# x as two float16 pieces turned by DMA, projections as three float16 products, mask turned by DMA, q read by ScalarE

## The reference

```python
xn = layernorm(x)
q = (xn @ Wq.T + bq) * 0.25; k, v = split(xn @ Wkv.T + bkv)        # 16 wide each
q = q.reshape(16, 16 * 512, 16)                                     # a plain reshape
attn = softmax(q @ k.T) @ v;  out = heads_back(attn) @ Wo.T + bo
gates = one_hot_of_the_best(xn @ w_gate)                            # 6 experts, top 1
tokens = A @ B                                                      # (6, 100, 256)
p = softmax((xn @ tokens.T) / 16)
delta = ((p @ (tokens @ wt.T + wt_b)) + xn) @ wd.T + wd_b, times scale
ffn = xn + log(sum_e exp(delta_e) * gates_e)
result = x + out + ffn
```

## Time and profile before

| | |
|---|---|
| median of 3 runs | 976.48 us (974.66 to 976.85) |
| span of the profiled execution | 972.5 us; no other time of it is given, and the median lies 4.0 us above the span |
| TensorE busy | 907.7 us (93%) |
| VectorE busy | 808.2 us (83%) |
| ScalarE busy | 682.1 us (70%) |
| GpSimd busy | 459.1 us (47%) |
| chain that ended last | TensorE 75%, VectorE 6%, DMA 6%, ScalarE 6%, GpSimd 3% |
| DMA | 76.07 MB, 78 GB/s on average |

### The profile page before, as it was taken

The page is one execution under the profiler, slowest core; times in us unless marked ns, Lnnn a source line. Parts: engine busy times, 40 slices in busy tenths (PEclk is TensorE's granted clock), DMA queues, the critical chain, the costliest instruction groups (busy, mean ns, idle before and its releaser), DMA issues.

```text
span 972.5 us, 17720 instructions
## 1 busy us (share of the span) xinstructions
PE 907.7 (93%) x5868; PEld 354.1 (36%) x5868; DVE 808.2 (83%) x1556; ACT 682.1 (70%) x1380; POOL 459.1 (47%) x567
## 2 busy tenths in 40 slices
PE   4889999999999999999999999999999999998976
PEld 3433333333434333343334333333333334332323
DVE  5688978889898888989888898989889898888814
ACT  1217777877777777777777777777777777777791
POOL 3654545554554555455444655444465544524200
PEclk9779999999999999999999999999999999999998
DMA  4230232422324242422423242242423223241120
GB/s 118 70 59 31 76 67 71 91 87 81 91 72 100 63 98 79 95 76 83 88 84 79 89 91 69 91 82 93 88 71 91 81 76 84 71 90 46 58 66 33
DMA packets 86192, 76.07 MB, mean 78 GB/s; under 512 B 18263, under 2 KB 70232, under 8 KB 86104
## 3 DMA queue, kind: packets, MB, share of 16 engines
q1 hardware_dynamic: 86104, 74.94, 29.9%
HBM read 39.28 MB, written 33.54 MB: 75 GB/s over the span
## 4 chain that ended last, share of the span: by engine, by line
PE 75%; DVE 6%; DMA 6%; ACT 6%; POOL 3%; issue 2%; SPq 2%; POOLq 0%; DVEq 0%
PE pO L349 22%; PE pA L331 14%; PE pB L336 8%; PE pA L470 6%; PE pA L412 6%; PE pA L488 5%; DVE M L750 3%; DMA o_parts<-OTr 3%; ACT P L597 3%; PE pA L472 3%; PE pA L402 3%; PE pB L392 2%; SPq L937 2%; PE pA L443 2%; DMA Rb<-l_parts 2%
## 5 line engine op out<-in xcount | busy, mean ns | idle before, releaser
L750 DVE TENSOR_REDUCE M<-pA 128x1 f32<-128x512 f32 x1024 | 652.4, 680 | 82.7 <-PE pA L331 80.9
L597 ACT ACTIVATE P<-pB 128x512 f32<-128x512 f32 x1002 | 553.5, 599 | 147.6 <-PE pB L336 143.1
L331 PE MATMUL pA<-K,Q 48*128 48x512 f16 x1024 | 316.8, 387 | 19.9 <-DVE M L750 10.3
L336 PE MATMUL pB<-Q,K 50*128 50x512 f16 x1002 | 307.3, 383 | 0.3 <-ACT P L597 0.3
L349 PE MATMUL pO<-P,VK 128*32 128x512 f32 x2048 | 272.8, 605 | 11.1 <-ACT P L597 7.9
L331 PEld LDWEIGHTS pA<-K,Q 48*128 48x128 f16 x1024 | 64.0, 94 | 323.2 <-DVE M L750 243.8
L887 POOL TENSOR_TENSOR On<-Op,Rb 128x512 f32<-128x512 f32 x31 | 39.9, 1288 | 146.9 <-DMA Rb<-l_parts 104.7
L873 POOL TENSOR_SCALAR Cz<-Cx 128x512 f32<-128x512 f32 x32 | 62.0, 1936 | 50.4 <-ACT Cx L579 50.4
L349 PEld LDWEIGHTS pO<-P,VK 128*32 128x32 f32 x2048 | 40.4, 108 | 108.3 <-issue 82.2
L412 PE MATMUL pA<-xT,wq 128*128 128x256 f32 x256 | 74.1, 416 | 1.3 <-ACT xT L541 0.7
L488 PE MATMUL pA<-wo,On 128*128 128x256 f32 x248 | 69.9, 407 | 4.3 <-DVE RL L763 2.5
(11 more groups left out here) (130 smaller groups left out, 865.7 us busy)
## 6 DMA issues: line engine op xcount, KB each, us to landing
o_parts<-OTr SPq DMA_DIRECT2D x62, 256.0 KB, 2.3
Q<-q_pieces SPq DMA_DIRECT2D x90, 128.0 KB, 4.1
X<-in_x SPq DMA_DIRECT2D x16, 512.0 KB, 3.9
q_pieces<-Qp SPq DMA_DIRECT2D x32, 256.0 KB, 2.1
out<-OUT SPq DMA_DIRECT2D x32, 256.0 KB, 3.1
Op<-o_parts SPq DMA_DIRECT2D x31, 256.0 KB
Rb<-l_parts SPq DMA_DIRECT2D x31, 256.0 KB
K<-KS SPq DMA_DIRECT2D x96, 16.0 KB, 1.8
```

The lines of the kernel that those rows point to most:

```text
L331: e.matmul(bank1("ab", t)[:, :], Q16[r:r + 48, b % 2, h, 128 * s:128 * s + 128], K16[r:r + 48, b % 3, :], start=True, stop=True).then_inc( ...
L336: e.matmul(bankB(t)[:, :], K16[r:r + 50, b % 3, 128 * i:128 * i + 128], Q16[r:r + 50, b % 2, :, 32 * hh:32 * hh + 32], start=True, stop=Tr ...
L597: e.activation(P[:, u % PR, :], bankB(u + LB)[:, :], ACT.Exp, scale=alpha).then_inc(S("e"))
L750: e.tensor_reduce(M[:, t // 32 % 2, t % 2, t % 32 // 2:t % 32 // 2 + 1], bank1("ab", t)[:, :], AX, ALU.max, negate=True).then_inc(S("mx"))
```

## The change

Each batch's normalised x is written by GpSimd times 1024 as a high and a low float16 piece (XP); SP issues one transposing DMA per batch that turns both pieces into xT (two for batch 0). The weights are scaled and split into two float16 pieces once (`scl`, `scd`). Every projection from x is three float16 products (high-high, high-low, low-high), over 512 columns at once for uk and q. The factors are taken out again where the results are read. The mask is turned by a DMA (`mkd`) instead of by TensorE and ScalarE. ScalarE reads q. The residual is worked out from x, not from XN. Slots are moved.

```diff
+PIECES = ((0, 0), (0, 1), (1, 0))
+    "root": -91.4, "refine": -90.2, "norm": -87.2, "pieces": -84.2, "xtd": -74.2,
+    "residual": 2.3, "q0": -57, "qe0": -55.4, "qs0": -53.8, "qw0": -50.2, "uk": -53, "uke": -51.4, "ks": -50.2,
+    "kd": -46.2, "vg": -49, "vge": -48.3, "q1": -45, "qe1": -43.4, "qs1": -42.2, "qw1": -38.2,
+    "vt": -41.1, "vte": -40.4, "gate": -38.8, "mask": -36.6, "mkd": -34.2,
-    "d0": -1, "dexp0": -0.4, "d1": 7, "dexp1": 7.6, "guard0": 8.8, "dlog0": 13.2, "radd0": 14.8,
+    "d0": -1, "dexp0": -0.4, "d1": 23, "dexp1": 23.6, "guard0": 24.8, "dlog0": 29.2, "radd0": 30.8,
-    "o0": 131, "fo0": 131.6, "o1": 163, "fo1": 163.6, "st0": 165.2, "o2": 179, "fo2": 179.6, "o3": 183,
+    "o0": 131, "fo0": 131.6, "o1": 155, "fo1": 155.6, "st0": 157.2, "o2": 163, "fo2": 163.6, "o3": 183,
...
+                        w.wait_ge(S(f"xt_{b % 2}"), turned(b))
+                        for k, (wp, xp) in enumerate(PIECES):
+                            for c in range(2):
+                                mm = e.matmul(bank1(f"q{g}", b)[:, :], wqP[:, wp, c, 128 * g:128 * g + 128],
+                                              xT[:, b % 2, :, xp, c, :], start=(k == 0 and c == 0), stop=(k == 2 and c == 1))
...
-                        for c in range(2):
-                            e.matmul(dst, xT[:, b % 2, c, 128 * t:128 * t + 128], wc[:, c, 0:C],
-                                     start=(c == 0), stop=False)
+                        for k, (wp, xp) in enumerate(PIECES):
+                            for c in range(2):
+                                e.matmul(dst, xT[:, b % 2, t, xp, c, :], wcP[:, wp, c, 0:C],
+                                         start=(k == 0 and c == 0), stop=False)
...
+                        e.activation(qf[:, g, :], bank1(f"q{g}", b)[:, :], ACT.Identity, scale=scl[:, 5:6],
+                                     bias=bq_s[:, g:g + 1]).then_inc(S(f"qe{g}"))
...
+                if (b := due("pieces", n)):
+                    w.wait_ge(S("xn"), 4 * b + 4)
+                    w.wait_ge(S(f"xt_{(b - 1) % 2}"), turned(b - 1))
+                    e.tensor_copy(XP[:, :, 0, :], XN[:, :, :]).then_inc(S("xh"))
+                    w.wait_ge(S("xh"), b)
+                    e.tensor_tensor(XP[:, :, 1, :], XN[:, :, :], XP[:, :, 0, :], ALU.subtract).then_inc(S("xl"))
...
+                if (b := due("xtd", n)) is not None:
+                    w.wait_ge(S("d"), 4 * (b - 1))
+                    if b:
+                        w.wait_ge(S("xl"), b)
+                    for i0, i1 in ((0, 2), (2, 4)) if b == 0 else ((0, 4),):
+                        if b == 0:
+                            w.wait_ge(S("xl0"), i1 // 2)
+                        e.dma_start_transpose(xT[:, b % 2, i0:i1].rearrange("p i k c t -> p (i k c) t"),
+                                              XP[:, i0:i1].rearrange("p i k n -> p (i k n)")).then_inc(S(f"xt_{b % 2}"), 16)
+
+                if (b := due("mkd", n)) is not None:
+                    w.wait_ge(S("mk"), b + 1)
+                    w.wait_ge(S("mk1"), 1)
+                    w.wait_ge(S("mm"), b)
+                    w.wait_ge(S("utm"), b)
+                    e.dma_start_transpose(mkT[:, :].rearrange("p (i t) -> p i t", t=128),
+                                          mk[:, :, :].rearrange("p i n -> p (i n)")).then_inc(S("mkd"), 16)
```

More of the change, by code:

```diff
@@ L73 @@
 PARTH = {"lr": 66.2, "or": 66.3, "rec": 68.8, "lw": 69.4, "rb": 72.2, "on": 78.3}
[L75 to L78, removed]
+PE_NAMES = ("ab", "pv", "rg", "bs", "bw0", "bw1", "w2", "uk", "q0", "q1", "vg", "vt", "s", "p", "a", "d0", "d1",
+            "d2", "d3", "mt", "o0", "o1", "o2", "o3", "sl0", "sl1", "oa0", "oa1", "oa2", "oa3", "ob0", "ob1", "ob2", "ob3")
+ACT_NAMES = ("root", "alpha", "bwe0", "bwe1", "w2e", "pieces", "qe0", "qe1", "vge", "vte", "sexp", "pte", "dexp0",
              "dexp1", "dexp2", "dexp3", "dlog0", "dlog1", "mte", "ex", "ot")
-DVE_NAMES = ("rng", "two", "scl", "stats0", "stats1", "stats2", "stats3", "aggr", "refine", "uke0",
-             "uke1", "qe00", "qe01", "qe10", "qe11", "gate", "smax", "ssum", "mm", "mx", "rec", "fo0", "fo1", "fo2",
+DVE_NAMES = ("rng", "two", "scl", "scd", "stats0", "stats1", "stats2", "stats3", "aggr", "refine", "pieces", "uke",
+             "gate", "smax", "ssum", "mm", "mx", "rec", "fo0", "fo1", "fo2",
              "fo3", "nl00", "nl01", "nl02", "nl03", "nl10", "nl11", "nl12", "nl13")
-POOL_NAMES = ("var", "refine", "norm", "residual", "ks", "qs0", "qs1", "mask", "utm", "snorm", "guard0", "guard1", "radd0",
+POOL_NAMES = ("var", "refine", "norm", "pieces", "w2s", "residual", "ks", "qs0", "qs1", "mask", "utm", "snorm", "guard0", "guard1", "radd0",
               "radd1", "ms", "on")
-SP_NAMES = ("load", "kd", "qw0", "qw1", "qread", "md", "ow", "lr", "or", "lw", "rb", "st0", "st1")
+SP_NAMES = ("load", "xtd", "mkd", "kd", "qw0", "qw1", "qread", "md", "ow", "lr", "or", "lw", "rb", "st0", "st1")
 def slots():
@@ L362, in _ @@
                     w.wait_ge(*before1("bs", 0))
-                    w.wait_ge(S("ones"), 5)
+                    w.wait_ge(S("ones"), 4)
                     w.wait_ge(S("two"), 1)
-                    e.matmul(bank1("bs", 0)[:, 0:3], one[:, :], fac[:, 0:3], start=True, stop=True).then_inc(S("bs"))
+                    e.matmul(bank1("bs", 0)[:, 0:7], one[:, :], fac[:, 0:7], start=True, stop=True).then_inc(S("bs"))
                 for h in range(2):
@@ new lines, in _ @@
+                for g in range(2):
+                    if (b := due(f"q{g}", n)) is not None:
+                        w.wait_ge(*before1(f"q{g}", b))
+                        w.wait_ge(S(f"xt_{b % 2}"), turned(b))
+                        w.wait_ge(S("wqp"), 2)
+                        for k, (wp, xp) in enumerate(PIECES):
+                            for c in range(2):
+                                mm = e.matmul(bank1(f"q{g}", b)[:, :], wqP[:, wp, c, 128 * g:128 * g + 128],
+                                              xT[:, b % 2, :, xp, c, :], start=(k == 0 and c == 0), stop=(k == 2 and c == 1))
@@ L417, in _ @@
                     w.wait_ge(*before2("vg", b))
-                    w.wait_ge(S("xte"), 2 * b + 2)
-                    for c in range(2):
-                        for i in range(4):
-                            mm = e.matmul(bank2("vg", b)[32 * i:32 * i + 32, 0:128], wc[:, c, V0:V0 + 32],
-                                          xT[:, b % 2, c, 128 * i:128 * i + 128], start=(c == 0), stop=(c == 1))
+                    w.wait_ge(S(f"xt_{b % 2}"), turned(b))
+                    w.wait_ge(S("wcp"), 2)
+                    for k, (wp, xp) in enumerate(PIECES):
+                        for c in range(2):
+                            for i in range(4):
+                                mm = e.matmul(bank2("vg", b)[32 * i:32 * i + 32, 0:128], wcP[:, wp, c, V0:V0 + 32],
+                                              xT[:, b % 2, i, xp, c, :], start=(k == 0 and c == 0), stop=(k == 2 and c == 1))
                     mm.then_inc(S("vg"))
@@ L428, in _ @@
                     e.transpose(bank2("vt", b)[:, 0:128], VGs[:, :], idf[:, :]).then_inc(S("vt"))
-                if (b := due("mk", n)) is not None:
-                    w.wait_ge(*before2("mk", b))
-                    w.wait_ge(S("mk"), b + 1)
-                    o = bank2("mk", b)[:, :].bitcast(BF16)
-                    for i in range(4):
-                        mm = e.transpose(o[0:ER, 128 * i:128 * i + 128], mk[:, i, :], idb[:, :])
-                    mm.then_inc(S("mkt"))
                 if (b := due("s", n)) is not None:
@@ L547, in _ @@
                     e.activation(VGs[:, :], bank2("vg", b)[:, 0:128], ACT.Identity,
-                                 bias=vgb[:, 0:1]).then_inc(S("vge"))
+                                 scale=scl[:, 4:5], bias=vgb[:, 0:1]).then_inc(S("vge"))
                 if (b := due("vte", n)) is not None:
@@ L556, in _ @@
                     e.copy(G[:, :, :], o[:, :, D:D + NE]).then_inc(S("gt"))
-                if (b := due("mke", n)) is not None:
-                    w.wait_ge(S("mkt"), b + 1)
-                    w.wait_ge(S("mm"), b)
-                    w.wait_ge(S("utm"), b)
-                    e.copy(mkT[0:ER, :], bank2("mk", b)[0:ER, :].bitcast(BF16)[:, 0:T]).then_inc(S("mke"))
                 if (b := due("sexp", n)) is not None:
```

243 lines of the change are left out of this document (137 added, 106 removed), and 7 rows, old and new, of tables (FIRST, SLOT).

## The result

The changed kernel takes 1034.57 us (median; 1032.56 to 1039.72), the kernel before on the same chip 975.57: a ratio of 1.0617, interval 1.0578 to 1.0655. The forecast was 943 us. Its span is 1030.8 us.

A forecast was written before the change was run, and what follows sets the result against it. TensorE's order of work was taken to bound a batch, VectorE about 5 us behind. Per batch -4.2 + 0.6 + 0.5 = -3.1; span 972.5 + 13 (start) - 46.5 = 939, with 4.0 more 943 us; range 918 to 984.

The forecast's parts named there:

- the turned DMAs: SP's queue: x's turn lands in 5 us, hidden under 13; Rb queued behind it is charged 0.5 us a batch.
- TensorE, -4.2 us a batch: TensorE's products: turns of x and mask go, q, uk and delta get cheaper in f16; -4.2 us a batch, to 50.7.
- rival 3: TensorE: f16 products don't stream at one column a cycle (weight loads); 4.1 us a batch at the end, about 972; chance 0.07.
- VectorE, 47.0: VectorE per batch: four q reads go, two uk reads become one at 0.689; busy time falls from 49.2 to 47.0 us.
- Rival 2: VectorE becomes the bound, 47.0 against TensorE's 50.7; 2 us a batch instead of 0.6, 963 us; chance 0.16.
- The 0.6 us for its order: Allowance per batch for places where VectorE runs behind TensorE, such as slots 12 to 15 and 56 to 59.
- ScalarE at most 0.78 for q's read: ScalarE: each of two q reads of 512 columns takes 0.78 us at most; net -0.2 a batch, counted as nothing.
- GpSimd, hidden: GpSimd between normalisation and En: +4.2 us a batch, pieces 0.611 and 1.155 per half; 1.6 us cover left, nothing charged.
- The turned x in 5 us: x's transposing DMA, 512 KB a batch, lands in 5 us, near the 3.9 of the plain load of equal size.
- Rival 1: Turned x late, or holding up what queues behind it, at q or output projection; about 1045 at 20 us; chance 0.19.
- Start, first pair near 44, batch 1's q near 54: Start: batch 0's q at about 25 us, first pair about 44, batch 1's q near 54; charged +13 us (8 to 20).
- Period 52.9: Time of one batch in the long middle, forecast 52.9 us after 55.99; wrong if above 54.

The follow-up runs named there:

- e14: Changed kernel with one unused tile of 416 bytes a partition ahead of xT, so Q16 begins at 70656, a multiple of 512: 985.4 us (1.0123).
- e13: e4 with one unused tile of 416 bytes a partition ahead of xT, so Q16 begins at 70656, a multiple of 512: 966.68 us (0.9924).
- e3: Changed kernel with batch 0's read of q put behind the turning of batch 0's mask on SP's queue: 1026.16 us (1.0533).
- e1: Changed kernel with kd, the six DMAs that place k, moved back to slot 23.8, behind the read of the softmax sums: 1018.35 us (1.0447).
- e4: Changed kernel with both moves, e1's of kd and e3's of batch 0's read of q: 1012.59 us (1.04).
- e9: Kernel before with one unused tile of 32 bytes a partition ahead of xT, so Q16 begins at 70176: 994.57 us (1.0228).
- e16: Kernel before with Q16 alone 32 bytes further (70176), every other tile at its place modulo 512: 997.37 us (1.0247).
- e5: e4 with the transposing DMAs of x and mask replaced by plain DMAs between the same tiles, nothing turned: 1008.96 us (1.0342).
- e18: e13 with the reciprocal and its result's write two slots later, and x's transposing DMA behind Rb: 985.63 us (1.0093).

## Why the prediction was wrong

The account of the 59 us, by the runs: the place of the tiles 49 (changed kernel against e14; Q16's, as argued above), the two slots on SP's queue 19 (e14 against e13: the first mask 8 by e3, so kd about 11 by difference; e1's 16 with e3's 8 make 24, e4 gives 22, so they overlap a little), and -7 to -9 for all the rest of the change (e13 against the kernel before in the same runs and in the first), against the -33 forecast.

- **What the prediction left out, and what decided:** it has no term for where the tiles lie. In its part on what bounds the kernel and in its turned DMAs, q's reads and o_parts stay as they were. They became 1.1 us slower, o_parts behind them 1.0 to 1.7 in the rows above, and its landing decides when VectorE may go on with the row maxima. In the kernel before Rc idled there too, 0.65 to 2.3 us, but TensorE waited for maxima at L331 for 3.4 us only between 160 and 880; the same misplacement made that 15.4 (e9) and cost 20 to 22 us (e9, e16). In the changed kernel the wait went from 31.4 (e14) to 52.5, and the mean clock from 1.00 to 0.96, where e9 still has 0.99. That these two, more of each wait and the half clock behind it, make up the 49 is argued from these figures; no run separates them.
- **The step "the turned DMAs", what it does delay:** it looked at Rb and at nothing else on SP. kd's new slot, in plain sight in the change, puts six DMAs with 3.7 to 4.5 us of SP's time ahead of Lc. Rc's wait for Lc is named nowhere. This is the step that failed within what the text did look at. What it did charge, 0.5 us a batch for Rb ahead of the output projection, is not seen there: no row of the changed kernel or of e13 has the projection wait for On. In e13 the lateness shows at the product that turns the maxima instead, where TensorE waits for GpSimd's M 11 times between 160 and 880 us, 6.5 us in all.
- **TensorE, -4.2 us a batch:** right in the prices: in e13, q's groups 1.40, uk 1.43, delta 0.76 (before, also behind a pair, 1.06): rival 3 is out. Its busy time fell by less. In the middle of e13 TensorE is busy 677.27 / 720 x 54.66 = 51.4 us a batch, after 54.3: -2.9. The forecast's 50.7 can't be set beside that, since it comes off the chain's sum of 54.9 and not off the 54.3 of busy time.
- **VectorE, 47.0:** e13 has 616.42 / 720 x 54.66 = 46.8. UK's read is 0.801, not the 0.689 taken. Rival 2 is not what happened: VectorE idles, it isn't full. The 0.6 us for its order did come about: behind uk's read TensorE waits 0.58 us for a maximum in each batch of e13 (447.89, 502.44). What it left out is again Rc.
- **ScalarE at most 0.78 for q's read:** 0.772. **GpSimd, hidden:** the cast takes 1.04 and the low piece 2.14, and En still idled 11.5 us in 12 cases for sR, 1.0 us each where 1.6 was forecast, so the cover held.
- **The turned x in 5 us:** 4.5, and e5 against e4 shows what turning costs the whole kernel: 1.04 against 1.0342, with intervals that overlap. Rival 1 had the right sign, "holds up what is queued behind it", but its mechanism, late turned data, is refuted by e5, and TensorE waits for xT nowhere between 160 and 880 us. That its 1045 us lies near the measured time is chance. "Advanced Engine Details and Errata", section X-Bar Transpose (TRN2), of the Trainium skill was nearer than "VectorE: DVE Perf Modes", section The three transpose paths: 512 KB turned in 4.5 us, plain in 3.1.
- **Start, first pair near 44, batch 1's q near 54:** 50.14 and 62.00. The work up to q was right (23.56 for 25). Missed: the mask's turn waits on SP behind the twelve reads; with e3 the first pair is at 43.89 and batch 1's q at 55.01.
- **Period 52.9:** 54.66 where both faults are mended. Left there: Rc's wait of 1.7 to 2.65 us at slot 52.8, and the chain through Rb at slot 24. e18 shows that they can't be traded by moving Rc and the turned x alone. They are not all of the 1.8 us: TensorE's time outside its busy time grew from 55.99 - 54.3 = 1.7 us a batch to 54.66 - 51.4 = 3.2, against the 1.1 that the forecast charged, which leaves 0.5; the other 1.3 lie in busy time that fell by 2.9 in place of 4.2. Why it did, with every price met, stays open (the ends of matmuls are modelled, so busy time is the weaker measure). Nor was each of the four parts of the change undone by itself, so what is left is not split among them.

e13_both_512 is the best version found: 0.9924 of the kernel before, interval 0.9894 to 0.9953, with all of the change kept but kd's slot and the first batch's read of q.

## What to carry to other kernels

A change that adds or resizes a tile also moves every tile behind it: before pricing anything else, work out the start address of each tile that DMAs with small packets write (512 bytes here; K16, written in pieces of 1024, landed in 1.8 us at either place), and keep it at a multiple of 256 bytes. Go through a shared queue by each step that is moved, own slot and new neighbours, and ask for each neighbour which engine stands in order behind its result. A row for an unchanged transfer that changed its landing time is the trail to follow.

## What the hardware showed that was not expected

- 512-byte packets into Q16 took 46 ns each with Q16 at a multiple of 512 bytes (the kernel before) and 63 at 96 beyond a multiple of 256 (the changed one); q's 128 KB reads landed in 4.1 to 4.3 us at 0 modulo 256 and in 5.2 to 5.3 at 32, 96 and 128 alike.
- Turning 512 KB of f16 in one DMA took 4.5 us and 1.7 to 3.3 us of SP's own time, the plain copy 3.1.
- In the changed kernel, after 2.44 us (459.51) and 2.46 us (493.83) in which TensorE got no work, its granted clock was 0.50 over the next 5 us; after 0.57 us (429.89) it was 1.00. The means over the middle are 0.96 in the changed kernel and 1.00 in e14 and e13.
